# Casting the down weights during gate and up, and asking for residual tiles two ahead in the down stage

## The reference, cut to what matters

```
x = x + attn(layernorm(x))              # Wq, Wk, Wv, Wo with biases
W = (w_int32 - 128) * scale[:, None]    # gate, up: (8192, 2048); down: (2048, 8192)
h = silu(layernorm(x) @ Wg.T) * (layernorm(x) @ Wu.T)
x = x + h @ Wd.T
```

## Time and profile before

| | |
|---|---|
| median of 3 runs | 2107.71 us (2096.15 to 2113.34) |
| profiled execution, its time | 2099.14 us |
| its span on the slowest core (6) | 2097.6 us (cores: 2073.0 to 2097.6) |
| PE, DVE, ACT, POOL busy on core 6 | 93%, 61%, 52%, 8% |
| HBM read, written | 394.64 MB, 60.82 MB |

### The profile page before, as it was taken

The page is one execution under the profiler, slowest core; times in us unless marked ns, Lnnn a source line. Parts: engine busy times, 40 slices in busy tenths (PEclk is TensorE's granted clock), DMA queues, the critical chain, the costliest instruction groups (busy, mean ns, idle before and its releaser), DMA issues.

```text
span 2097.6 us, 34047 instructions; the slowest of 8 cores (2073.0 to 2097.6 us)
## 1 busy us (share of the span) xinstructions
PE 1955.4 (93%) x11408; PEld 964.5 (46%) x11408; DVE 1280.6 (61%) x1953; ACT 1099.0 (52%) x1243; POOL 159.5 (8%) x245
## 2 busy tenths in 40 slices
PE   5998998896999899999999999999999999779995
PEld 3544554553555565444444444444444444224442
DVE  5614665564666577666666666666666566556664
ACT  2326887785888783544444544444543444135340
POOL 2001010111101110000000000000000000010002
PEclk9999999998999999999999999999999999889998
DMA  9529978878977877645555445445442976666656
GB/s 242 167 41 166 123 105 104 127 123 126 145 102 141 140 134 235 135 101 112 118 103 113 89 81 93 89 81 93 89 81 61 306 218 198 168 218 195 205 176 185
DMA packets 81879, 289.89 MB, mean 138 GB/s; under 512 B 10544, under 2 KB 10544, under 8 KB 67760
## 3 DMA queue, kind: packets, MB, share of 16 engines
q0 software_dynamic: 22528, 152.06, 43.5%
q1 hardware_dynamic: 59184, 135.66, 21.3%
HBM read 394.64 MB, written 60.82 MB: 217 GB/s over the span
## 4 chain that ended last, share of the span: by engine, by line
PE 70%; DMA 22%; DVE 3%; issue 2%; POOL 1%; ACT 0%; SPq 0%; DVEq 0%; POOLq 0%; ACTq 0%
PE PS_B L171 19%; DMA arena<-xt 17%; PE PS_C L171 16%; PE PS_A L171 15%; PE PS_D L171 10%; DMA arena<-x2d 3%; PE PS_C L167 3%; DVE arena L205 3%; PE PS_A L167 2%; PE PS_B L167 2%; PE PS_D L167 1%; DMA x2d<-arena 1%; POOL arena L213 1%; DMA arena<-wv 1%; PE PS_D L182 1%
## 5 line engine op out<-in xcount | busy, mean ns | idle before, releaser
L205 DVE TENSOR_TENSOR arena<-arena 128x1024 bf16<-128x1024 bf16 (+3 forms) x1004 | 532.2, 571 | 186.1 <-ACT arena L192 73.6
L171 PE MATMUL PS_D<-arena 128*128 128x256 bf16 (+1 forms) x2598 | 526.6, 322 | 65.3 <-DVE arena L205 46.2
L171 PE MATMUL PS_B<-arena 128*128 128x512 bf16 (+1 forms) x2461 | 548.6, 362 | 26.9 <-DVE arena L205 26.6
L192 ACT ACTIVATE arena<-arena 128x1024 bf16<-128x1024 bf16 x416 | 416.0, 1048 | 243.6 <-PE PS_C L167 122.3
L171 PE MATMUL PS_C<-arena 128*128 128x512 bf16 (+1 forms) x2131 | 471.1, 357 | 5.0 <-DVE arena L205 4.2
L171 PE MATMUL PS_A<-arena 128*128 128x512 bf16 (+2 forms) x2009 | 432.7, 355 | 10.8 <-DMA arena<-wv 7.8
L171 PEld LDWEIGHTS PS_B<-arena 128*128 128x128 bf16 (+1 forms) x2461 | 217.3, 98 | 304.2 <-issue 83.1
L192 ACT ACTIVATE arena<-PS_B 128x1024 bf16<-128x1024 f32 (+1 forms) x203 | 193.9, 955 | 283.0 <-PE PS_B L167 282.8
L171 PEld LDWEIGHTS PS_D<-arena 128*128 128x128 bf16 x2598 | 233.3, 99 | 226.0 <-issue 139.1
L171 PEld LDWEIGHTS PS_C<-arena 128*128 128x128 bf16 (+1 forms) x2131 | 185.4, 98 | 238.9 <-issue 51.2
L171 PEld LDWEIGHTS PS_A<-arena 128*128 128x128 bf16 (+1 forms) x2009 | 173.4, 98 | 222.6 <-issue 52.2
(11 more groups left out here) (48 smaller groups left out, 946.4 us busy)
## 6 DMA issues: line engine op xcount, KB each, us to landing
arena<-dws SPq DMA_DIRECT2D x288, 256.0 KB, 3.6
dws<-dwt POOLq DMA_DIRECT2D x32, 1024.0 KB, 19.9
arena<-gwt POOLq DMA_DIRECT2D x32, 1024.0 KB, 8.1
arena<-uwt POOLq DMA_DIRECT2D x32, 1024.0 KB, 7.9
arena<-xt SPq DMA_DIRECT2D x16, 1024.0 KB, 11.8
arena<-wq POOLq DMA_DIRECT2D x32, 512.0 KB, 15.9
arena<-wo POOLq DMA_DIRECT2D x6, 2048.0 KB, 27.6
arena<-xt SPq DMA_DIRECT2D x32, 256.0 KB, 16.9
```

Source lines behind the costliest of these rows:

```text
L171: e.matmul(o, ll, rr, start=a, stop=b, skip_group_check=k))
L192: e.activation(o, i, f, bias=b, scale=s)
L205: getattr(e, n)(*a).then_inc(DVE, 1))
```

## The change

1. The DMA `dws<-dwt` leaves the attention loop. At the end of every `gu_unit`, behind `load_raw(u + 4)`, POOL issues half a tile (256 rows: 1 MB read, 0.5 MB written), 64 in all. The semaphore DWC becomes two, one for the tiles of each nu, and `ring_loads` waits for them at the first tile of each nu, where one wait stood ahead of the ring.
2. The order of the residual tiles is written out in a list, XSEQ. `xl_load(k)` asks for tile k; tiles 0 and 1 are asked for ahead of the down stage, and each `add_x2` asks for tile k + 2 right behind its add.
3. The output entries move. For nu 0, slot 3 finishes only the four V tiles; the T tiles are scaled and finished, with the four X tiles, in slot 0 of nu 1, where an entry is taken after every step and not every second one. `evict` of slot 3 at nu 0 adds the bank of PSUM to T directly. For nu 1, the four V and then the four T entries run in slot 3, in another order than before. The scale tiles of nu 1 are loaded inside slot 0 of nu 1.

```diff
-            if k < 256 and k % 8 == 1:
-
-                xd_dwc = g_dma("DWC", dws[k // 8, :, :], dwt[k // 8, :, :])
...
                 load_raw(u + 4)
+
+            rows = slice(256 * up, 256 * up + 256)
+            xd_dwc[p // 16] = g_dma("DWC%d" % (p // 16), dws[p, rows, :],
+                                    dwt[p, rows, :])
...
+                if sl == 0 and st == 0 and qt == 22:
+                    y_wait("DWC%d" % nu, xd_dwc[nu])
...
+        def xl_load(k):
+            tm, nu, n = XSEQ[k]
+            e = k % 2
+            g_wait(*(xl_free[k - 2] if k >= 2 else ("PE", pe_m[(63, 6)])))
+            c = nu * 1024 + n * 512
+            xl_dma[k] = ("XL%d" % e, g_dma("XL%d" % e, XL(e),
+                                           x2d[tm * P:(tm + 1) * P, c:c + 512]))
+
+        def add_x2(view, tm, nu, n, tok):
+            k = xl_n[0]
             xl_n[0] += 1
+            assert XSEQ[k] == (tm, nu, n)
+            v_wait(*xl_dma[k])
             v_wait(*tok)
+            t = ("DVE", v_op("tensor_tensor", view, view, XL(k % 2), ALU.add,
+                             inc=True))
+            xl_free[k] = t
+            if k + 2 < len(XSEQ):
+                xl_load(k + 2)
             return t
...
+                later_ops.extend(fin_v(i) for i in range(4))
+                if nu == 1:
+                    later_ops.extend(pre_t(i) for i in range(4))
+            elif nu == 0:
                 for i in range(4):
+                    w = [pe_done[("D", i)], ds_dma[0], out_sem[("X", i)]]
+                    x = vtt(X2P(i), gb("D", i), DS(0), ALU.mult, w)
+                    t_tok[i] = vtt(T_(i), T_(i), gb("D", i), ALU.add, [t_tok[i]])
+                    bank_free[("D", i)] = [t_tok[i]]
+
+                    def fin_t(i=i):
+                        t = scale(T_(i), i, 0, t_tok[i])
+                        x2_out("T", i, T_(i), i, nu, 0, t)()
+                    later_ops.append(fin_t)
+                    x_tok[i] = x
+                for i in range(4):
+                    later_ops.append(x2_out("X", i, X2P(i), 4 + i, nu, 0, x_tok[i]))
+                later_ops.append(lambda: ds_load(1, 0))
...
-            if later_ops and st % 2 == 0 and st < 15:
+            if later_ops and (st % 2 == 0 or (nu == 1 and sl == 0)) and st < 15:
                 later_ops.pop(0)()
...
-            if nu == 0 and sl == 3 and st == 15:
-                ds_load(1, 0)
+            if nu == 1 and sl == 0 and st == 4:
+
                 ds_load(1, 1)
```

More of the change, by code:

```diff
@@ L110, in build_program @@
                    + ["RW0", "RW1", "RW2", "RW3", "HSP", "HRL0", "HRL1", "HRL2",
-                      "DS0", "DS1", "DWC", "PE", "ACT", "DVE", "GP"]
+                      "DS0", "DS1", "DWC0", "DWC1", "PE", "ACT", "DVE", "GP"]
                    + ["RG%d" % i for i in range(13)]
@@ L1096, in build_program @@
         dve_t11, dve_t22, dve_hm = {}, {}, {}
-        xd_hsp, xd_hrl = {}, {}
+        xd_hsp, xd_hrl, xd_dwc = {}, {}, {}
         def product(u, j, bank, first, last):
@@ L1483, in out_store @@
                 s, out_d[tm * P:(tm + 1) * P, c:c + 512], view))
-        def add_x2(kind, i, view, tm, nu, n, tok):
-            e = xl_n[0] % 2
-            xl_n[0] += 1
[L1489 to L1493, removed]
-            v_wait(*tok)
-            t = ("DVE", v_op("tensor_tensor", view, view, XL(e), ALU.add, inc=True))
-            xl_free[e] = t
+        XSEQ = []
+        for nu_ in range(2):
+            XSEQ += [(i, nu_, 1) for i in range(4)]
+            XSEQ += [(4 + i, nu_, 1) for i in range(4)]
+            XSEQ += [(i, nu_, 0) for i in range(4)]
+            XSEQ += [(4 + i, nu_, 0) for i in range(4)] if nu_ == 0 else []
+        xl_dma = {}
+        def xl_load(k):
[7 more added lines that the diff above has]
+            k = xl_n[0]
+            xl_n[0] += 1
+            assert XSEQ[k] == (tm, nu, n)
+            v_wait(*xl_dma[k])
+            v_wait(*tok)
+            t = ("DVE", v_op("tensor_tensor", view, view, XL(k % 2), ALU.add,
[3 more added lines that the diff above has]
+                xl_load(k + 2)
             return t
@@ L1500, in f @@
             def f():
-                t = add_x2(kind, i, view, tm, nu, n, tok)
+                t = add_x2(view, tm, nu, n, tok)
                 out_store(kind, i, view, tm, nu, n, t)
@@ L1555, in evict, with fin_v @@
                     bank_free[("D", i)] = [t_tok[i]]
-                def tail(i):
+                def fin_v(i):
                     def f():
@@ L1560, in f, with pre_t @@
                         x2_out("V", i, V_(i), 4 + i, nu, 1, v_tok[i])()
-                    def f2():
+                    return f
+                def pre_t(i):
+                    def f():
                         t_tok[i] = scale(T_(i), i, 0, t_tok[i])
-                        t_tok[i] = add_x2("T", i, T_(i), i, nu, 0, t_tok[i])
-                    return [f, f2]
-                for i in range(4):
-                    later_ops.extend(tail(i))
+                        t_tok[i] = add_x2(T_(i), i, nu, 0, t_tok[i])
+                    return f
+                later_ops.extend(fin_v(i) for i in range(4))
+                if nu == 1:
+                    later_ops.extend(pre_t(i) for i in range(4))
+            elif nu == 0:
+                for i in range(4):
+                    w = [pe_done[("D", i)], ds_dma[0], out_sem[("X", i)]]
[10 more added lines that the diff above has]
+                later_ops.append(lambda: ds_load(1, 0))
             else:
                 xv = {}
[L1570 to L1575, removed]
+                for i in range(4):
+                    g_wait(*out_sem[("V", i)])
+                    xv[i] = ("XL%d" % (2 + i), g_dma(
+                        "XL%d" % (2 + i), V_(i),
+                        x2d[(4 + i) * P:(5 + i) * P, nu * 1024:nu * 1024 + 512]))
                 for i in range(4):
@@ L1578, in evict @@
                     t = vtt(X2P(i), gb("D", i), DS(0), ALU.mult, w)
[L1579 to L1593, removed]
+                    t2 = vtt(T_(i), T_(i), X2P(i), ALU.add, [t, t_tok[i]])
+                    out_store("T", i, T_(i), i, nu, 0, t2)
+                    t = vtt(X2P(i), X2P(i), V_(i), ALU.add, [xv[i]])
+                    out_store("X", i, X2P(i), 4 + i, nu, 0, t)
+        x_tok = {}
         ring_loads(-1)
@@ L1596, in build_program @@
         ds_load(0, 1)
+        xl_load(0)
+        xl_load(1)
         forms(0)
@@ L1609, in build_program @@
             step(g)
-            if later_ops and st % 2 == 0 and st < 15:
+            if later_ops and (st % 2 == 0 or (nu == 1 and sl == 0)) and st < 15:
                 later_ops.pop(0)()
             if st == 15:
+                assert sl != 0 or not later_ops
                 evict(nu, sl)
-            if nu == 0 and sl == 3 and st == 15:
-                ds_load(1, 0)
+            if nu == 1 and sl == 0 and st == 4:
                 ds_load(1, 1)
```

## The result

The change took the kernel from 2110.53 us to 2031.03 us (medians of four runs each; ratio 0.9641, 95% interval 0.9575 to 0.9707). The profiled execution took 2030.23 us. One of the four runs of each kernel lay apart, 2177 us before and 2195 us after (there with the cores of one die at a granted clock of 0.90), and the ratio is worked out without it. The forecast was 2013, the range 1994 to 2042.

A forecast was written before the change was run, and what follows sets the result against it. Full DMA engines were taken to hold TensorE up in attention, late residual tiles in down. Core 6: 2097.6 - 51 + 3 - 42 = 2007.6; core 3: 2015; slowest near 2011 of span, forecast 2013 us, range 1994 to 2042.

The forecast's parts named there:

- part 1 in attention: Attention, core 6: without the cast, DMA share falls from 0.84 to 0.40 and queueing waits go, -51 us.
- the clock's 10: Attention, core 6: 10 us come back from lower granted clock after stalls, counted within the -51 us.
- Slowest core between 25 and 51: Attention: the slowest core gains between 25 us, if core 3's loss is the floor of queueing, and 51 us.
- Part 1 in gate and up: Gate and up: half a tile costs 4.7 us, a unit's DMA 11.3 of 12.07 us, share 0.93, later 0.88; it fits, barely.
- 3 us for instruction fetches: Gate and up: an allowance of +3 us for instruction fetches that share full DMA engines, as in attention.
- rival (d): Gate and up: half a tile costs the full 10 us, a unit 16.1 us, +240, about 2250 us; chance 0.03.
- Part 2 and 3, the down stage: Down, core 6: moved entries and reordered residuals gain -18, -9, -10 and -5 us, sum -42.
- 2 for one late tile: Slot 3 of nu 0: 2 us within a sum of 32 against 50.3 us, -18.
- rival (b): Down: landing rises to 10 us since faster slots draw ring tiles quicker, 303 GB/s; +21, 2034 us; chance 0.10.
- x2d waits under 2 us each: Sign for the profile after: VectorE's waits for x2d in slot 3, 8.04 us before, under 2 us each.
- three links at 4 us together: Slot 0 of nu 1: three residual links, 8.2 us each at 7 us landing against 6.9 for two steps, cost 4 us.
- the forecast 5: End of the kernel: VectorE finishes some 3 us after the last matmul, not 8.2, so -5 us.

The follow-up runs named there:

- its control: The change with only the ring cut from 13 to 11 slots; ratio 0.9656 to the kernel before, runs 2033.8 to 2037.9 us.
- the cast alone: The kernel before with only the cast moved into gate and up and the two DWC waits, down stage as before; ratio 0.9827 to the kernel before.
- the double cast: The change with every half tile cast a second time into a DRAM tensor nobody reads; 2296.5 us, ratio 1.0884 to the kernel before.
- whole tiles: The change with a whole tile cast at the end of each up unit, not half a tile every unit; 2028.04 us, ratio 0.9667 to the kernel before.
- down alone: The change with the cast DMA put back in the attention loop, keeping the new down stage; ratio 0.9808 to the kernel before.

## Why the prediction came out as it did

**What bounds the kernel, and part 1 in attention: right.** Core 6 was forecast to win 51 us less 3 and won 48.3 ahead of down, all of it ahead of gate and up. The waits named went, the short ones stayed: idle TensorE ahead of gate and up fell by 39.5 us, where the sum had 41.3, and the rest, 8.8, stands for the clock's 10. The DMA share fell from 0.84 to 0.47 and not to 0.40: a tile had cost some 8.5 us of the engines, not 9.5. All cores now begin down within 5 us. "Slowest core between 25 and 51" came out at 47 (1628.2 to 1581.0), median core 33.

**Part 1 in gate and up: right.** The half tile cost 4.2 us in the first part and less later, against 4.7; the share is 0.87 and then 0.75, where the sum had 0.93 and 0.88. The 3 us for instruction fetches did not appear. The sum adds up engine times as if a transfer cost the same at any load. That held here, but with a second half tile a unit takes 16.7 us and not 14.2, so the margin towards rival (d), a half tile above 7.7 us, says less than it seems: the more is moved, the more each transfer costs.

**Part 2 and 3, the down stage: right in sign, mis-sized: 26 of 42 us.** Of the 16 us between them the end holds 7.1, slot 3 of nu 0 5.6, slot 0 of nu 1 2.8 and slot 3 of nu 1 1.8, and slots 0 to 2 of nu 0 give 1.4 back. In slot 3 of nu 0 the step that failed is the sum "27.6 us of matmuls, 2.7 for the banks that evict frees one after the other (unchanged), and 2 for one late tile". It priced only the residual chain. Slot 3 needs 303 GB/s of ring tiles, and that stood in rival (b) as a reason for slower landing of residuals, not as a wait of its own for ring tiles.

The runs show such a wait. With residuals four ahead and no x2d wait, but the same bytes, slot 3 did not get shorter (40.0 against 38.9 in its control). With half the ring bytes and the same residuals it did (33.6, where the change has 37.5), and without the residual loads too (32.7). With all ring bytes, but no residuals or stores in it, it took 30.9. So the slot is held up by the sum of its transfers, which start late since the engines stand still during evict. It took 37.9 us against 32, and the sign written down, x2d waits under 2 us each, failed too: they are 4.07 and 3.05.

In slot 0 of nu 1 the landing was as taken, 5.9 to 7.8 us with a median of 7.1. The sum had three links at 4 us together; the trace has six waits for x2d, 8.6 us, and the gain was 6.2 and not 9. In slot 3 of nu 1 the gain was 8.2 and not 10. Rival (b) at 2034 came nearest in time, with half of the true cause: its landing of 10 us was 9.0 in slot 3 of nu 0, but it had no wait for ring tiles. The range held; the forecast itself missed by 18 us.

**The end: wrong by 7 us.** This is the largest single miss. VectorE finished 5.6 us after the last matmul (8.2 before), so the forecast 5 was 2.6. And something else grew. POOL's last issues and its last record, the DRAIN at the end of the program, in the kernel before and in the change:

```profile
2090.37 1.14 POOL L138 DMA_DIRECT2D out<-arena  x2 [0.93 <-DVE arena L205]
...
L1625 POOLq DRAIN  x1: 6426/6426/6426, 2090.9 to 2090.9; - x1
```

```profile
2011.24 1.14 POOL L138 DMA_DIRECT2D out<-arena  x2 [0.93 <-DVE arena L205]
...
L1656 POOLq DRAIN  x1: 11081/11081/11081, 2011.8 to 2011.8; - x1
```

From POOL's last issues to the end of the span are 7.2 us before and 11.9 after, the same 11.9 on all eight cores, and the DRAIN (its length in ns stands behind x1) fills nearly all of it: 6.4 to 7.4 us before, 11.1 after. On core 6 of the change it ends 8 us after the last store has landed. It is 11.1 us with the cast alone too, 8.8 without residual loads (9.5 on one core), 7.7 with the double cast and 9.8 with whole tiles. With down alone it is 6.4 on five cores and 10.4 to 10.8 on three, and with the ring cut to 11 it is 11.1 on six and 12.4 and 12.8 on two. So it changes with POOL's list of DMAs, but neither their number nor the list alone sets it: 32 casts give 6.4 in attention and 9.8 in gate and up, and cores with the same list differ. What the DRAIN waits for stays open.

**The median.** I had taken 7.6 us off for queueing that goes. The runs behind the ratio lie at 2028.28 to 2031.82 for the change and at 2096.15 to 2113.34 for the kernel before, and the profiled run of the change is 0.8 under the median of the four, as assumed.

## What to carry to other kernels

Work moved from a stage that is full of DMA to one that is full of matmuls is free as long as the DMA engines keep up with all cores running: here it was at a share of 0.75 to 0.87, and with the moved part doubled it cost 4 us a unit. Measure that by doubling the moved part, since the cost of a transfer at low load understates it. When a wait for one stream is removed, ask what rate the other streams of that stage then need, and whether they stand still at some time just before. To tell a late transfer from too many transfers, ask earlier for the same bytes in one run and for fewer bytes in another. Cores that no longer drift apart ask for their traffic together; that this costs time is likely here, but not shown.

## What the runs showed of the hardware

By estimate from the DMA shares, one cast of half a tile took 4.2 us of all DMA engines beside 2 MB of weight reads per 12.07 us, and 4.9 to 5.4 us when the engines were at a share of 1.01. Memory traffic, read and written, was 325 GB/s for each core in the first units of gate and up without any wait of TensorE. Ring tiles of 256 KB landed in 4.6 us on the whole, in 10.9 to 14.8 in slots 3 with residuals or stores beside them, and in 4.4 in a slot 3 without. The residual tiles of one stretch landed in 7.7 us from ScalarE's hardware queue and in 7.5 from POOL's software queue: the queue made no difference. The DRAIN that ends POOL's list took 6.4 to 12.8 us, up to 8 us longer than the landing of its last DMA.
